# A ring of seven probability slots, TensorE's work placed by its lead over ScalarE, and 204 exponential blocks on VectorE instead of 170

## What is computed

```python
h = layernorm(x) * (1 + ca) + sa
q, k = split(h @ Wq.T), split(h @ Wk.T)      # 32 half heads of size 8
v = split(h @ Wv.T)                          # 16 heads of size 16
aw = softmax(q * 8**-0.5 @ k.T)              # 4 x 32 x 2048 x 2048
aw = aw[:, :, 0] - lam * aw[:, :, 1]
attn = rmsnorm(aw @ v) * subln_w * (1 - LAMBDA_INIT)
x = x + ga * (attn @ Wo.T)
h = layernorm(x) * (1 + cb) + sb
x = x + gb * (h @ (ternary(Wf) * scale).T)
```

## Time and profile before

| | us |
|---|---|
| median of 3 runs | 3692.14 |
| lowest, highest | 3689.13, 3692.22 |
| profiled execution | 3690.33 |
| its span, first to last instruction | 3688.6 |
| granted TensorE clock, mean | 0.994 |

### The profile page before, as it was taken

How to read it: one execution, slowest core, us unless ns; L and a number is a source line. 1 busy time by engine, 2 the same in 40 slices (tenths; PEclk the granted TensorE clock), 3 DMA queues, 4 the chain that set the end, 5 groups by cost and what they waited for, 6 DMA issues and landing times.

```text
span 3688.6 us, 76325 instructions
## 1 busy us (share of the span) xinstructions
PE 3406.7 (92%) x32302; PEld 810.0 (22%) x32302; DVE 2298.7 (62%) x3502; ACT 3577.7 (97%) x2808; POOL 332.8 (9%) x229
## 2 busy tenths in 40 slices
PE   8999898899899999999989999999998999989998
PEld 5111111122122222222212222222221222211222
DVE  6676877764556666556365665656546566577665
ACT  5999999999999999999999999999999999999998
POOL 3010100000010100100001010010100000000001
PEclk9999999999999999999999999999999999999999
DMA  5110110111101111100111101111012011000000
GB/s 192 27 43 27 31 30 21 35 29 41 38 26 36 43 40 34 53 23 28 40 46 49 29 22 40 40 47 35 20 43 65 28 36 28 16 24 15 20 21 26
DMA packets 103696, 136.85 MB, mean 37 GB/s; under 512 B 9916, under 2 KB 88716, under 8 KB 103340
## 3 DMA queue, kind: packets, MB, share of 16 engines
q1 hardware_dynamic: 102524, 131.01, 12.5%
q10 hardware_dynamic: 816, 0.79, 0.1%
HBM read 72.50 MB, written 59.19 MB: 36 GB/s over the span
## 4 chain that ended last, share of the span: by engine, by line
ACT 48%; PE 22%; issue 19%; DVE 7%; POOL 0%; ACTq 0%; DVEq 0%; POOLq 0%
ACT probs L1031 48%; PE ps L1176 12%; PE ps L1148 6%; PE ps L1063 1%; PE ps L1071 1%; DVE d_y L1516 1%; DVE d_y L1523 1%; DVE wmod_sb L1529 1%; DVE wmod_sb L1534 1%; DVE wmod_sb L1533 1%; DVE wmod_sb L1528 1%; POOL seg_rs L957 0%; DVE wmod_sb L1516 0%; PE ps L1057 0%; DVE a_qk L1459 0%
## 5 line engine op out<-in xcount | busy, mean ns | idle before, releaser
L1031 ACT ACTIVATE probs<-ps 128x1536 f32<-128x1536 f32 (+1 forms) x2732 | 3540.7, 1538 | 55.5 <-PE ps L1148 53.5
L1176 PE MATMUL ps<-probs,values 128*32 128x512 f32 x14728 | 2053.5, 607 | 10.9 <-DVE wmod_sb L1534 9.6
L1148 PE MATMUL ps<-queries,keys 25*128 25x512 f16 x7680 | 1006.1, 386 | 216.7 <-ACT probs L1031 186.2
L1148 PEld LDWEIGHTS ps<-queries,keys 25*128 25x128 f16 x7680 | 251.3, 91 | 2046.9 <-ACT probs L1031 1817.5
L1598 DVE STREAM_TRANSPOSE seg_t<-ps 128x512 f32<-128x512 f32 x127 | 91.1, 717 | 546.8 <-PE ps L1176 546.8
L1176 PEld LDWEIGHTS ps<-probs,values 128*32 128x32 f32 x14728 | 301.0, 108 | 424.2 <-issue 393.2
L957 POOL TENSOR_TENSOR seg_rs<-seg_ms,neg_half 128x16 f32<-128x16 f32 x64 | 185.6, 2899 | 1431.4 <-DVE seg_ms L1611 1431.4
L1516 DVE TENSOR_SCALAR d_y<-ps 128x512 f32<-128x512 f32 x240 | 164.8, 686 | 204.8 <-PE ps L1148 193.7
L1529 DVE SCALAR_TENSOR_TENSOR wmod_sb<-wmod_sb 128x1024 f32<-128x1024 f32 x170 | 208.2, 1225 | 5.8
L1534 DVE SCALAR_TENSOR_TENSOR wmod_sb<-wmod_sb,gates 128x1024 f32<-128x1024 f32 x170 | 208.2, 1225 | 5.8
L1533 DVE SCALAR_TENSOR_TENSOR wmod_sb<-wmod_sb,d_y 128x1024 f32<-128x1024 f32 x170 | 207.6, 1221 | 3.8
(11 more groups left out here) (181 smaller groups left out, 1687.7 us busy)
## 6 DMA issues: line engine op xcount, KB each, us to landing
v_scr<-a_v SPq DMA_DIRECT2D x16, 1024.0 KB, 5.8
values<-v_scr SPq DMA_DIRECT2D x29, 512.0 KB
queries<-q_scr SPq DMA_DIRECT2D x116, 96.0 KB
keys<-k_scr SPq DMA_DIRECT2D x116, 96.0 KB
e_x<-in_x_dram SPq DMA_DIRECT2D x18, 512.0 KB, 5.2
attn_scr<-seg_o SPq DMA_DIRECT2D x254, 32.0 KB
e_attn<-attn_scr SPq DMA_DIRECT2D x31, 256.0 KB, 3.7
out_dram<-e_y SPq DMA_DIRECT2D x15, 512.0 KB, 3.1
```

The costliest lines, as they stand in the source:

```text
L1031: nc.scalar.activation(probs[:, s % PRING, at, :], ps[:, base + at.start:base + at.stop:at.step, :], ACT.Exp, scale=1.0 / SQUARE).then_inc ...
L1148: last = nc.tensor.matmul(ps[:, score_bank(n), :], keys[buf][at, u * P:(u + 1) * P], queries[buf][at, tc * CH:(tc + 1) * CH], start=True, ...
L1176: last = nc.tensor.matmul(pv[row:row + VW, :], values[buf][:, n % SEG_BANKS // HEADS, j // 2, :], probs_of(n), start=(i == 0), stop=(i == ...
```

## The change

The ring has 7 slots instead of 6 (the announcement spoke of 8; the code sets 7). `schedule()` keeps a ledger of TensorE's lead over ScalarE in nanoseconds: each slot adds 1008, or 583 where VectorE takes one of its banks; a group takes 998 and a piece 430; what is left over is cut to 606 or 181. A group is placed when the lead covers it or when it is three slots late, a piece when the lead covers it or when more than six wait. A step opens no sooner than three slots after the one before it closed. Pieces fall due one unit earlier. The blocks' banks stand at places 14 and 15 of the groups. `shared()` allows a second block in more segments: 204 blocks instead of 170. VectorE's loop goes by slots: score reads first, then the segment's sums in the slot of its last group, evacuations, the parts of the blocks by the new table `WORK_AT`, then at most one follow-up, if no score read falls in the next one or two slots; the layer norms are split in two follow-ups (`e_stats`, `e_apply`).

```diff
@@ -68,9 +68,13 @@
     HEADS = 4
     WIDE = 3
     RING = 2
-    PRING = 6
+    PRING = 7
     OPEN = 4
     BEHIND = 2
+    SPARE = 3
+    APART = 3
+    LONG = 6
+    ROOM_THREE, ROOM_TWO, LEAD_THREE, LEAD_TWO, GROUP, PIECE = 1008, 583, 606, 181, 998, 430
     VW = 32
     PARTS = 2
...
     def part(p):
 
-        return [p // 2 * NB + u for u in ((6, 7, 8, 9) if p % 2 else (0, 1, 2, 4))]
+        return [p // 2 * NB + u for u in ((5, 6, 7, 8) if p % 2 else (0, 1, 2, 3))]
 
@@ -180,7 +184,7 @@
     SEG_PAIRS = ALL_SEGS // 2
 
     D_UNITS = ((4, 6), (8, 10))
-    D_AT = (12, 15)
+    D_AT = (14, 15)
     D_LINKS = 6
 
@@ -195,7 +199,7 @@
         light = {("a", 0): 1, ("a", 1): 1, ("a", 6): 2, ("a", 7): 2, ("e", 0): 2, ("e", 2): 1, ("e", 3): 1, ("e", 4): 2, ("e", 5): 2}
         steps = {step[0:3:2] for u, step in steps_of(k // SEGS).items() if u // NB == seg}
         normed = norm_at(k // SEGS) // NB == seg and k // SEGS + 1 < (B - 1) * GP
-        return 2 if sum(light.get(step, 4 if b else 2) for step in steps) <= 2 and not normed else 1
+        return 2 if sum(light.get(step, 3) for step in steps) <= 5 and not normed else 1
 
     SHARED = [shared(k) for k in range(ALL_SEGS)]
@@ -235,6 +240,17 @@
 
     D_BANKS = [bank_id(k, u, j) for k in range(ALL_SEGS) for places in d_places(k) for u, j in places]
     D_ORDER = {n: i for i, n in enumerate(D_BANKS)}
+
+    WORK_AT = {}
+    for k in range(ALL_SEGS):
+        reads = [slot_of(n) for places in d_places(k) for n in [bank_id(k, u, j) for u, j in places]]
+        at = []
+        if SHARED[k] == 1:
+            at = [reads[1], reads[1] + 2, reads[1] + 4]
+        elif SHARED[k] == 2:
+            at = [reads[1], reads[2], reads[3], reads[3] + 2, reads[3] + 4, reads[3] + 6]
+        for i, s in enumerate(at):
+            WORK_AT.setdefault(s, []).append((k, i // 3, i % 3))
     assert D_BANKS == sorted(D_BANKS) and len({slot_of(n) for n in D_BANKS}) == len(D_BANKS)
 
@@ -267,29 +283,34 @@
     def schedule():
 
         groups_at, steps_at, closed_at = [], [], {}
-        g, queue, rest = 0, [], False
+        g, queue, rest, closed, lead = 0, [], False, -APART, 0
         for s in range(ALL_SLOTS):
             made, done = [], []
-            if g < ALL_SEGS * NB and NEEDS[g] <= s - BEHIND and not rest:
-                made.append(g)
-                g += 1
-            rest = bool(made) and g % NB == 0
+            mixed = any(n in D_ORDER for n in slot_banks(s))
+            lead += ROOM_TWO if mixed else ROOM_THREE
             for n in slot_banks(s):
                 if n % HEADS == HEADS - 1:
                     step = steps_of(n // HEADS // BODY).get(n // HEADS % BODY)
                     if step:
                         queue.append(step)
-            last = s % BATCH_SLOTS == BATCH_SLOTS - 1
-            room = 0 if made else 2
-            if made and (len(queue) > 3 or unit_of(s) % NB >= 13):
-                room = 1
-            if s >= slot_of((ALL_SEGS - 1) * SEG_BANKS):
-                room = 2
-            while queue and (last or room > 0):
-                room -= 2 if queue[0][0] == "m" else 1
+            last = s % BATCH_SLOTS == BATCH_SLOTS - 1 or s >= slot_of((ALL_SEGS - 1) * SEG_BANKS)
+            behind = s - BEHIND - NEEDS[g] if g < ALL_SEGS * NB else -1
+            pressed = len(queue) > LONG
+            if behind >= 0 and not rest and (lead >= GROUP or behind >= SPARE):
+                made.append(g)
+                g += 1
+                lead -= GROUP
+            rest = bool(made) and g % NB == 0
+            while queue and (last or lead >= PIECE or pressed and not done and not mixed):
+                opens = queue[0][0] == "m" or queue[0][3] == 0
+                if opens and s < closed + APART and not last:
+                    break
+                lead -= PIECE
                 done.append(queue.pop(0))
                 if done[-1][3] == PIECES - 1:
                     closed_at.setdefault(unit_of(s), []).append((s, *done[-1][0:3]))
+                    closed = s
+            lead = min(lead, LEAD_TWO if mixed else LEAD_THREE)
             groups_at.append(made)
             steps_at.append(done)
...
@@ -1488,16 +1510,19 @@
                 V.scalar_tensor_tensor(wo_gated[:, :, :], wo[:, :, :], subln_sb[:, 0:1], wo_gated[:, :, :], ALU.mult, ALU.mult)
                 V.tensor_tensor(wf_gated[:, :, :], wf[:, :, :], wf_gated[:, :, :], ALU.mult).then_inc(e_gated, 1)
 
-            def e_norm(job):
+            def e_stats(job, i):
                 norm_stats(Chain(dve, e_chain, job * E_LINKS), e_x2, e_ve, e_var)
+
+            def e_apply(job, i):
                 norm_apply(e_x2, e_rstd, e_rstd_done, job, e_normed)
 
             def follow(kind, job, i):
 
                 if kind == "a" and 2 <= i < 6:
-                    a_bounds(job, i - 2, job % NC)
-                elif kind == "e" and i == 1:
-                    e_norm(job)
+                    return [(a_bounds, job, i - 2)]
+                if kind == "e" and i == 1:
+                    return [(e_stats, job, i), (e_apply, job, i)]
+                return []
 
             d_blocks = [d_probs[:, r, :, :].rearrange("p h c -> p (h c)") for r in range(2)]
...
                     wait_alone(dve, exact_done, runs + 1, dve_passed)
                     dve.reg_add(exact_runs, exact_runs, 1)
 
...
+                before, followed = b * BATCH_UNITS - 1, []
+                for s in range(b * BATCH_SLOTS, (b + 1) * BATCH_SLOTS):
+                    unit = unit_of(s)
+                    body, u, seg, v = unit // BODY, unit % BODY, unit // NB, unit % NB
+                    first, before = unit > before, unit
+                    for n in slot_banks(s):
+                        if n in D_ORDER:
+                            share_read(n)
+                    for k in range(b * GP * SEGS, (b + 1) * GP * SEGS - 1):
+                        if GROUP_SLOT.get((k + 1) * NB - 1) == s:
+                            segment_sums(k // SEGS, k % SEGS)
+                    for slot, kind, job, i in CLOSED_AT.get(unit, ()):
+                        if slot == s:
                             if kind == "m":
                                 if i == CRIT + 1:
                                     dve.wait_ge(m_stored, job * (NC * DMA))
...
                                 a_evacuate(job, i, job // NC, job % NC)
                             else:
                                 e_evacuate(job, i)
...
+                            followed += follow(kind, job, i)
+                    for k, j, part in WORK_AT.get(s, ()):
+                        (share_round, share_middle, share_end)[part](k, j)
+                    if followed and not any(n in D_ORDER for t in range(s + 1, s + (2 if followed[0][0] in (e_stats, e_apply) else 3)) for n in slot_banks(min(t, ALL_SLOTS - 1))):
+                        task, job, i = followed.pop(0)
+                        task(job, i)
+                    if not first:
+                        continue
+                    if u == M_TURN[0] - 18 and body % GP == GP - 1 and b < B - 1:
+                        link = m_means(b + 1)
+                        m_sizes(link)
+                    if v == 5 and seg > 0 and (seg % 2 == 0 or seg == ALL_SEGS - 1):
+                        segment_norms((seg - 1) // SEGS, (seg - 1) % SEGS)
+                    if u == 8 and (body % GP == 0 and b > 0 or body == LATE):
+                        gate_weights(b - 1 if body % GP == 0 else b)
+                    if u == norm_at(body) and body + 1 < (B - 1) * GP:
+                        followed += [(a_stats, body + 1 + NC, 0), (a_apply, body + 1 + NC, 0)]
+                    if halved(body, u) and v == 11:
+                        last_sums(0)
+                    if halved(body, u) and v == 13:
+                        last_norms(0)
+                for task, job, i in followed:
+                    task(job, i)
+                if b < B - 1:
+                    segment_sums((b + 1) * GP - 1, SEGS - 1)
 
             last_sums(1)
             last_evacuate(0, 1, e_x, a_x, False)

```

62 lines of the change are left out of this document (7 added, 55 removed).

## The result

The changed kernel takes **3670.57 us** (median of 5 runs, 3666.31 to 3673.28), the kernel before 3689.31 in the same comparison (3687.18 to 3692.22): ratio **0.994**, 95% interval 0.993 to 0.995. I had forecast 3628, with a range of 3606 to 3662. The sign was right, the size was not: 19 us of the 64 came. The profiled execution took 3667.38 us; where the traces are compared, this one stands beside 3690.33. Of the executions behind the ratios that follow one is left out: a slow one of run 1, 5745 us at a granted clock of 0.892.

The account below looks back on a forecast made before the run. ScalarE's exponentials were taken as the bound: 3494.8 us without stalls plus 37 of stalls made a 3531.8 loop; with 76.1 ahead, 17.8 behind and small additions outside the span, 3628 us, range 3606 to 3662.

Parts of the forecast that it names:

- What bounds the kernel: ScalarE's exponentials bound the loop: 1.343 us per three-bank slot, 0.92 per two-bank slot, plus 71 us of stalls.
- Part 1: 34 more blocks go to VectorE, giving 412 two-bank slots instead of 344: -28.8 us of ScalarE's work.
- Part 2: Groups and pieces placed by TensorE's lead: 59 us of stalls fall to about 3, -56 us; at least -30.
- Part 3: Stalls unchanged in both kernels, at batch starts, batch 2's branch, the last gate weights and the loop's first slots: 12 us.
- Part 4: New stalls at normalizations behind the second Wo product: +16 us, bounds 0 to +32; query and key bounds in batch one: +2.
- job 10: Output tile at slot 2263: late normalization and segment sums make TensorE late three times, 2.6 us together.
- Part 5: TensorE's clock drops after long pauses: about half of seven new pauses cost one more microsecond, +4 us.
- The ring: Larger probability ring: 0 us by itself; it buys the freedom to postpone groups.
- A: Rival: stalls change place, as VectorE is loaded in the last batch with fixed order; 3650 to 3670 us, chance 0.18.
- C: Rival: VectorE bounds the 84 two-block segments, losing 2 us each, 168 us; 3779 us, chance 0.06.
- D: Rival: the change does not do what it says; result within 0.2% of before, chance 0.04.

Follow-up runs that it names:

- run 1: Changed kernel with the old rule of shared() put back, so 170 VectorE blocks and 344 two-bank slots: 3658.97 us, ratio 0.990.
- run 5: Changed kernel without the second block in 13 segments, at or right before the one with the last piece of e1; 191 blocks: 3648.62 us, ratio 0.989.
- run 6: Changed kernel without the second block in 13 other segments, mostly right behind the one with the last piece of e1; 191 blocks: 3674.6 us, ratio 0.996.
- run 8: Changed kernel with the old schedule() and the old rule of shared(), so 170 blocks: 3698.1 us, ratio 1.002.
- run 4: Changed kernel with VectorE reordered: no follow-up in a slot holding part of a block, last body's gate weights at unit 12 instead of 8: 3652.4 us, ratio 0.989.
- Run 10: Changed kernel with a ring of 6 probability slots instead of 7: 3723.23 us, ratio 1.008.
- run 11: Changed kernel with run 4's edits, and the normalization put behind segment sums due within three slots, except jobs 9 and 11; 204 blocks: 3628.73 us, ratio 0.983.
- run 9: Changed kernel with the old schedule() and its 204 blocks kept: 3778.17 us, ratio 1.023.
- run 7: Run 5's kernel with the two VectorE edits of run 4 added: 3634.76 us, ratio 0.985.

## Why the prediction was wrong, point by point

**What bounds the kernel**: right. Without a stall ScalarE's slots take 1.343 and 0.92 us in the traces of these kernels, and nearly all the rest is time in which it waits for the scores.

**Part 1** (34 blocks): right to the tenth, 28.8 us less work. But I called their cover "over 1300 us free", an average. At 13 places the free time behind the block was already taken, and there a block costs more than it brings. Runs 5 and 6 show it.

**Part 2** (placement by lead, -56): the mechanism is right and carries the result. With 170 blocks the planner brought 44 us of stalls (80.8 to 36.5, runs 8 and 1), inside my bounds of 30 to 59. Of small stalls, under 0.5 us each, 35 are left in the changed kernel, 11 us in all, where I had 3; most stand where a read is late behind odd sums and not behind a group.

**Part 3** (what stays): the three pauses at the batch starts came as forecast, and the first stall behind each is 1.17, 1.44 and 0.92 us, where I had about 1.3. The 5 us at batch 2 I had put into both kernels, and there I was wrong: the first three exponentials of batch 2 have 4.9 us of stalls before and none in the changed kernel. All three kernels with 170 blocks have them (4.9, 4.8 and 5.4 us), the others 1.4 at most; no run shows why. Together the starts cost 8.1 us, not 10. The gate weights were called unchanged, 1.6 us. They cost 9.0: VectorE comes to them earlier in its new order than their load is done. I had costed a wait at nothing that in the earlier trace rows had only just been covered.

**Part 4** (new stalls at the norms, +16; bounds, +2): the step that failed, with 40.0 and about 11 us. I had the place and the chain right: for job 10 I put the end of the transpose 7.1 us behind the start of slot 2263, and it came at 7.06. Two things made the term too small. First, I did not carry job 10's working over to its neighbours. Jobs 0, 4, 8 and 13 stood at no more than 0.35 each and cost 3.6, 3.7, 2.9 and 4.1, 13 of the 24 us missing. In them the last piece of e1 stands seven slots behind the block's last read, not eight as in job 10, and the next segment's first group five slots behind the piece and not four. From that read to that group it is 12 slots in both cases, and VectorE's chain through block, normalization and transpose is the same. Job 8, in order of time:

```profile
2791.39 0.39 PE L1169 MATMUL ps<-queries,keys 25*128 25x512 f16 x3
...
2802.77 0.69 DVE L1500 TENSOR_TENSOR e_x<-ps,e_x 128x512 f32<-128x512 f32 x1
...
2808.71 1.06 PE L1197 MATMUL ps<-probs,values 128*32 128x512 f32 x8 [1.62 <-DVE seg_t L1622]
```

TensorE begins the slot of the last read (2084) at 2791.39, VectorE has ended the block 11.35 us later, as at job 10 (11.34), and TensorE's group waits 1.62 us (job 10: 1.61). At jobs 0 and 4 VectorE ended 11.8 us behind that slot, and the wait was 2.40. So the forecast's own sum for job 10, done for these four, would have shown a full pause in each. Even my upper bound of +32 lay under the 40.0. Second, I took each as TensorE's lateness alone; most of the long ones cost a second stall (part 5). The bounds of q and k were mis-sized as well: a 2 us item between a block's first part and its next read, which I had counted in "a few segments"; run 4 took 10 us away there.

**Part 5** (clock, +4): right in kind, too small. In the loop of the changed kernel there are 15 stretches at the 1.2 GHz level, in the loop of before 8 (one at its very start left out in both). Thirteen stalls of over 1.5 us were followed within four slots by others of 1.3 us on average, 16.7 us in all, and at 12 of the 13 such a stretch begins; some 15 of the 16.7 us lie inside the table's 40.0 and 9.0, the others in batch 0. I had about 1 us for a pause that hits, which was a little low; above all, nearly all of them hit and not half.

The Trainium skill, "TensorE: Matmul & The Clock Gate", Part 1, says that the clock follows how busy TensorE has lately been. The row from 1113.90 agrees; priced for each long pause, as I did there, 7 us would still have been short, since there were 13 pauses and not seven.

**The ring**: I gave it 0, and said that what it buys is the freedom of part 2. Run 10 gives that freedom its price: 53 us.

**The rivals.** By time it is A, "stalls change their place" (3650 to 3670), at its upper end, and its test in the profile came true: TensorE's waits for score reads grew by 12.4 us (23.4 to 35.8). But A's reason was VectorE's load in the last batch. Only 37 of the 78 us lie there, and runs 5, 6 and 11 show order and place: at the full load of 204 blocks the time is 3628.7 once the bounds and gate weights have moved and the sums no longer stand behind a normalization that waits. That this is my forecast of 3628 does not confirm it: the forecast was for a kernel without these edits. C (3779 from VectorE as the bound in each two-block segment) did not happen; with the old planner the same kernel does take 3778 (run 9). There 68 of 183 us of stalls are at the norms. TensorE waits 53.9 us for finished blocks, most of them near the norms, and 35.6 us for score reads; how the other 114 us of stalls divide between its own work and VectorE's was not separated. With the new planner the same 34 blocks cost 12 us, so VectorE's load alone, which was C's mechanism, does not make this number. D falls by part 1's count. The range was also drawn too narrow for its own bounds: those of parts 2 and 4 together (+26 and +16) reach 3670, and it ended at 3662.

What stays open: 4 us between the sum of the two cures and run 7; why the 5 us at the start of batch 2 went; why jobs 0 and 4 had VectorE 0.4 us later than jobs 8 and 13 (a late read of a bank stands in the block, but no run tests it). The price of the low clock was read from the traces, and no kernel varied it alone.

## What to carry to other kernels

Where an engine has a fixed program, ask of each item that waits (here 1.1 us for GpSimd, 5 us for a DMA) what stands finished behind it: moving a wait behind ready work gained 24 us with the same instructions, moving the item earlier in time lost 10. When work is added to an engine that is free 30% of the time, price it at the places where it lands, since 13 blocks ahead of an item cost 26 us more than 13 behind it. And when one case of a pause is worked out, do the same sum for every other case, from the last thing that ties the late engine down to the first thing that waits for it: here the place of the piece between them moved, the distance did not, and four of 15 jobs were put at 0.35 us that cost 3 to 4.

## What the runs showed of the hardware

- TensorE idle for 2.40 us was followed by 3.4 us at a granted clock of 0.51, in which a group of eight products took 1.94 us instead of 1.06. Of 13 stalls of over 1.5 us 12 had such a stretch behind them; the largest stall in the four slots that followed was 0.7 to 1.5 us, over 1 us in 8 of the 13.
- With one probability slot fewer ScalarE lost 0.76 us at 70 of the 88 slots whose last reader stands in the same place of TensorE's program, where I had expected 0.2 to 0.5.
